# GpSimd takes six eighths of the second payload side beside some units of a bitonic sort, and half beside the others

## The reference, cut to what matters

```python
for i in range(E):                                     # 16 experts
    gate_feature = hidden_states * pe[i] @ gate_w + gate_b
    gate_weight, gate_idx = jax.lax.top_k(gate_feature, K)       # K = 384 of 768
    gate_weight = jax.nn.softmax(gate_weight, axis=-1)
    gathered = jnp.take_along_axis(hidden_states, gate_idx, axis=-1)
    y = y + _moe_mlp(gathered * gate_weight, eg_w[i], eu_w[i], ed_w[i])
```

## Time and profile before

| | us | |
|---|---|---|
| median of 3 runs | 6788.27 | 6777.15 to 6796.1 |
| the profiled execution | 6784.21 | span 6782.4 |
| TensorE matmul busy | 5769.8 | 85% |
| VectorE busy | 5283.0 | 78% |
| GpSimd busy | 3697.6 | 55% |
| ScalarE busy | 2751.2 | 41% |

### The profile page before, as it was taken

How to read it: one execution, slowest core, us unless ns; L and a number is a source line. 1 busy time by engine, 2 the same in 40 slices (tenths; PEclk the granted TensorE clock), 3 DMA queues, 4 the chain that set the end, 5 groups by cost and what they waited for, 6 DMA issues and landing times. The chain is left out here.

```text
span 6782.4 us, 73995 instructions
## 1 busy us (share of the span) xinstructions
PE 5769.8 (85%) x16753; PEld 3057.5 (45%) x16753; DVE 5283.0 (78%) x6633; ACT 2751.2 (41%) x4419; POOL 3697.6 (55%) x3692
## 2 busy tenths in 40 slices
PE   7979989788888878888888888888888888889988
PEld 5545545344444444444444444444444444445554
DVE  3012002499999999999999999999999999998840
ACT  0000000245555545454545454545454555554431
POOL 2325015265766656565656565656565656666630
PEclk9989999899999999999999999999999999999989
DMA  3356238100000000000000000000000000001001
GB/s 89 106 139 179 101 110 196 41 15 16 20 15 15 14 15 14 15 14 15 14 15 14 15 14 15 14 23 6 29 0 29 14 15 14 15 28 35 15 35 51
DMA packets 118084, 261.01 MB, mean 38 GB/s; under 512 B 39164, under 2 KB 49922, under 8 KB 117682
## 3 DMA queue, kind: packets, MB, share of 16 engines
q1 hardware_dynamic: 70322, 180.18, 7.5%
q0 software_dynamic: 47360, 77.17, 5.1%
HBM read 222.43 MB, written 34.58 MB: 38 GB/s over the span
## 5 line engine op out<-in xcount | busy, mean ns | idle before, releaser
L1204 PE MATMUL mask_ps<-key,neg_ident 125*125 125x480 f32 (+7 forms) x4128 | 1884.8, 575 | 599.4 <-DVE key L1612 596.1
L1493 ACT COPY mask_ps<-key 125x960 f32<-125x960 f32 (+7 forms) x1152 | 955.0, 829 | 1733.8 <-DVE pay L1652 1072.8
L1313 POOL TENSOR_TENSOR pay<-pay_side,pay 125x480 int32<-125x480 int32 (+5 forms) x1120 | 1102.2, 984 | 882.9 <-DVE pay L1635 878.4
L1204 PEld LDWEIGHTS mask_ps<-key,neg_ident 125*125 125x125 f32 x4128 | 726.9, 192 | 1503.0 <-DVE key L1612 1048.3
L1305 POOL TENSOR_TENSOR pay_side<-pay 125x480 int32<-125x480 int32 (+5 forms) x1120 | 1098.0, 980 | 481.6 <-DVE pay L1652 346.5
L1635 DVE COPY_PREDICATED pay<-mask_ps,pay 125x960 f32<-125x960 int32 (+6 forms) x1120 | 1236.5, 1104 | 53.3 <-PE mask_ps L1204 29.1
L1602 DVE TENSOR_TENSOR key<-mask_ps,key 125x960 f32<-125x960 f32 (+6 forms) x1120 | 1089.8, 973 | 48.8 <-PE mask_ps L1204 38.4
L1612 DVE TENSOR_TENSOR key<-mask_ps,key 125x960 f32<-125x960 f32 (+6 forms) x1120 | 1089.6, 973 | 0.0
L1204 PE MATMUL mask_ps<-key_top,neg_ident 125*125 125x480 f32 (+3 forms) x1472 | 609.2, 543 | 184.6 <-DVE key_top L1612 170.8
L1652 DVE COPY_PREDICATED pay<-mask_ps,pay_side 125x480 f32<-125x480 int32 (+5 forms) x1120 | 710.6, 634 | 4.8 <-DVE pay L1635 2.9
L1151 PE MATMUL slot_ps<-w_exp,hid 128*125 128x384 f32 x1920 | 685.9, 496 | 9.4 <-issue 9.4
(11 more groups left out here) (190 smaller groups left out, 5855.9 us busy)
## 6 DMA issues: line engine op xcount, KB each, us to landing
w_rel<-L_gnn_W SPq DMA_DIRECT2D x16, 2304.0 KB, 23.3
w_exp<-L_ffn_ed_w SPq DMA_DIRECT2D x16, 2304.0 KB, 8.4
messages_dram<-y_out SPq DMA_DIRECT2D x16, 1875.0 KB
w_exp<-L_ffn_eg_w SPq DMA_DIRECT2D x16, 1152.0 KB, 5.4
w_exp<-L_ffn_eu_w SPq DMA_DIRECT2D x16, 1152.0 KB, 7.8
root_w<-L_gnn_root SPq DMA_DIRECT2D x2, 2304.0 KB
w_exp<-L_ffn_sg_w SPq DMA_DIRECT2D x4, 1152.0 KB, 5.9
w_exp<-L_ffn_su_w SPq DMA_DIRECT2D x4, 1152.0 KB, 8.7
```

The costliest lines, as they stand in the source:

```text
L1204: last = pe.matmul(mask, neg_ident[0:TP, 0:TP], operand, start=False, stop=True, skip_group_check=True)
L1313: pool.tensor_tensor(second, shares(pay_was(turn, u), turn, u)[1].bitcast(I32), first, ALU.subtract).then_inc(pays_taken, 1)
L1493: act.copy(seed_of(turn, u), compared(turn, u)[0]).then_inc(seeded, 1)
```

## The change

`shares` gives GpSimd 6/8 instead of 4/8 of the second side in those units of `REGULAR` that are in the set `turn.free`. The set is computed from the schedule of the loop's turns: units in which GpSimd has no `weigh` and nothing of the list that `beside_all` gives it with a lag of 2. The same set holds in all 15 turns of `REGULAR`, also in the first and the last, whose lists of other work are different. Units from `streams` on stay at 3/8, `OPENING` and `CLOSING` as they were. No instruction is added, removed or reordered; in each unit whose cut moves, the add and the take of GpSimd become longer, and VectorE's second copy and ScalarE's saving copy become shorter.

```diff
@@ -126,6 +126,7 @@
     def __init__(self, units, streams, first, earlier=None, times=1):
         self.units, self.n, self.streams, self.first = units, len(units), streams, first
         stages = [s for s, _, _ in units]
+        self.free = set()
         self.joint = [stages.index(s) for s in JOINT if s in stages]
@@ -199,7 +200,7 @@
     dim = next(d for d in range(1, len(view.shape)) if view.shape[d] > 1)
-    eighths = 4 if u < turn.streams else 3
+    eighths = 3 if u >= turn.streams else 6 if turn is REGULAR and u in turn.free else 4
     cut = view.shape[dim] - max(1, view.shape[dim] * eighths // 8)
@@ -1055,6 +1056,19 @@
+        def asked(flag, parts):
+
+            return do if flag else nothing, ([],) if flag else (), parts
+
+        asked_early = [asked(True, parts) for parts in down_parts(KD)]
+        asked_early += [asked(half == 1 and t + 2 < NT, parts) for t, half, parts in halves_of(gate_parts, range(AHEAD))]
+        asked_late = [asked(False, parts) for parts in turn_parts]
+        asked_late += [asked(n % 2 == 1, parts) for n, parts in enumerate(mixed_parts(KK, KD))]
+        asked_late += [asked(False, parts) for _, _, parts in halves_of(gate_parts, range(AHEAD, NT))]
+        asking = beside_all(REGULAR, asked_early, asked_late, 2)
+        REGULAR.free = {u for u in range(REGULAR.n) if not WEIGH <= u < WEIGH + NT
+                        and all(work is nothing for work, _ in asking.get(u, []))}
```

## The result

| | before | after |
|---|---|---|
| median of the runs, us | 6788.97 (6777.15 to 6796.1, 4 runs) | 6723.94 (6713.35 to 6737.39, 4 runs) |
| profiled execution, us | 6784.21 | 6728.35 (span 6726.6) |
| mean of the loop's 13 turns, us | 324.67 | 320.61 |

The ratio is 0.9908, with a 95% interval of 0.9892 to 0.9925: the change makes the kernel 65 us faster. The forecast was 91 us (6697 us, in a range of 6656 to 6755). The direction and the mechanism held; a good quarter of the gain is missing, and the experiments look for it. The two profiled executions stand 55.9 us apart. 52.9 us of that come from the 13 loop turns (4.07 us each), 1.1 from turn 1, 4.4 from turn 15 and what follows; 2.5 us are lost because the sorts start that much later.

The account below looks back on a forecast made before the run. VectorE was taken as the bound. Its 8.77 us a turn, less 0.77, 0.77, 0.37, 0.50 and 0.15, left 6.21, 80.7 us in 13 turns; with 5 each for turns 1 and 15, 91 us: 6697 us, range 6656 to 6755.

Parts of the forecast that it names:

- What bounds the kernel: In a regular turn of 324.2 us VectorE is the bound, busy 314.9 us, 97%.
- The count and GpSimd's side: 37 of 93 units change; GpSimd pays 32.3 us more a turn, and 720 columns take it about 1.7 us.
- VectorE's saving: Its second copy gets shorter by 1.14 ns a column: 7695 columns, 8.77 us a turn if all showed.
- End of the turn: At unit 90 GpSimd's take, 0.50 us longer, is on the path and VectorE's 0.27 us is lost: 0.77 us.
- Units 39 to 45: Unit 39's longer take heads GpSimd's queue and delays the seed of unit 45: 0.77 us off the saving.
- Unit 75: Unit 74's longer take delays the add that unit 75's first payloads wait for: 0.37 us off the saving.
- Start of the turn: TensorE runs masks and products back to back; waits for masks of units 2 and 7 swallow 0.50 us.
- so this rule stays out of the sum: VectorE's masked copies run beside GpSimd unheld, so whole-instruction exclusion on the shared port pair was given no cost.
- TensorE as bound in the early units: Rival: savings in units 1 to 38 are all lost, a turn gains 3.1 us, 6742 us; chance 0.11.
- Nothing: Rival: GpSimd lands on the path in about 12 places, so nothing to measure, say 6785 us; chance 0.08.
- the slower kernel: Rival: GpSimd's longer add or take comes too late beside busy units, 6931 us if all 27 are hit; chance 0.06.
- The engines exclude each other: Rival: GpSimd's added 32.3 us a turn pushes VectorE by as much, less 8.8: 7141 us; chance 0.01.

Follow-up runs that it names:

- the kernel where GpSimd does not stand in the way, the kernel that beats both: The changed kernel with the negation moved to ScalarE and units 39, 74, 89 and 90 kept at 4/8: 6674.06 us, ratio 0.9830.
- the two kernels of 317.2 us: The changed kernel with GpSimd's old short instructions, some payloads unmoved (6673.4 us); and with the negation on ScalarE, units 39, 74, 89, 90 at 4/8 (6674.06 us).

## Why the prediction was right or wrong

**What bounds the kernel: right.** A turn in which VectorE saves 7.7 us (314.9 to 307.2) is 4.4 us shorter, and 6.8 (324.2 to 317.4) in the kernel where GpSimd does not stand in the way.

**The count and GpSimd's side: right.** 37 units; 30.7 us more a turn (32.3 forecast); 1.65 us for 720 columns (1.7, taken from the slope of the operation's two sizes); adds waited for 1.5 us a turn, under 2.

**VectorE's saving: slightly too large.** By the starts of the units 1.08 ns a column in place of 1.14, 8.3 instead of 8.77 us a turn: 0.46 us.

**The subtracted places.** End of the turn: 0.77 forecast, 0.77 measured (5.20 to 4.43). Units 39 to 45: 0.77 forecast, and 2.70 to 1.69, 1.01, measured, since the seed of unit 44 is late as well. Unit 75: 0.4 to 0.8 as forecast. Start of the turn: 1.35 of savings less 0.50 are 0.85 us by unit 10, measured 0.98 in this short turn and 0.51 in the long one; The prediction has TensorE back to back there. It is so only from unit 3 on; before each of the first three masks of the turn it pauses over 2 us, in before too. Missing: unit 90's mask, where the turn falls back by 0.28 us.

**The step that failed** is "so this rule stays out of the sum". I weighed the port rule on the masked copies only, and for them the trace bears me out: the copy of 240 columns takes 439 ns, while GpSimd is busy three quarters of the turn. I did not go through VectorE's other instructions. One of them, the negation, reads and writes SBUF with one input; it stood in the trace of before at 0.38 us and ended with GpSimd's add. It is held 0.84 us longer in after, 10.9 us in 13 turns. The Trainium skill (SBUF — State Buffer, section Who interferes with whom) lists `tensor_scalar`, which the negation is, among the VectorE operations that can take the port pair shared with GpSimd if their operands meet certain conditions; the engine that issues first keeps the pair for its whole instruction, and the other is blocked. This case agrees: GpSimd's add starts first, and the negation ends 0.02 to 0.03 us behind it in before, in after and in the kernels with unit 38 even and with unit 38 alone. That it is this lock, and not another, is read from the ends and from the Trainium skill, not measured apart.

**An assumption I never wrote down** was that TensorE's clock stays as it is. The seven long turns, less the shorter first one, put after's mean 0.8 us above the 319.8 of the short ones; before's falls put its mean 0.4 above its steady 324.2; 0.4 net.

**The sum by turn:** 6.21 forecast and 4.07 measured, 2.14 short; by these terms 0.84 (held) + 0.46 (a column's price) + 0.24 (seeds) + 0.28 (unit 90's mask) + 0.4 (clock) = 2.2. The remaining differences nearly cancel. These are losses read one by one from the traces of before and after. They aren't what a repair brings: the negation taken off VectorE brought 0.26 us. In 13 turns 28 us; turn 1 gained 1.1 instead of 5 us, turn 15 4.4 of 5, and 2.5 are lost before the sorts. That is 35 of the 35 us between 91 and the 55.9 of the profiled executions; the medians stand 9 us further apart. I can't say why turn 1 gained so little: its length was a bound's middle, not read from rows.

**The rivals.** TensorE as bound in the early units: false (experiment with the first 39 units). Nothing, and the slower kernel: false for the whole, true for the places on the path, where three units alone cost 29 us. The engines exclude each other: false for the masked copies, true for the one instruction. The price of the clock was in none of them. With it, 50 us are lost to four units and a negation of five elements.

**Open:** why, after the same pause of 2.04 us at unit 55, the clock falls in one turn and not in the next, and why a change at unit 39 bears on it. One difference stands in the trace of after: the long stretch over the turn's border ends 17.2 to 17.4 us into each of the five short turns and 17.7 to 18.5 us into each of the seven long ones. It can't be the whole answer, since in the two kernels of 317.2 us it ends at 17.6 to 18.2 us, behind their first loop turn, and no fall follows. Extra products to keep TensorE busy in the pause were not tried, and neither was a delay that moves VectorE's work without a longer pause of TensorE.

## What to carry to other kernels

Before work goes to an engine with idle time, list the places where its results are waited for and leave these out: here 33 changed units bring 116 us together with a moved negation, and 37 bring 65. Look at every instruction of the relieved engine beside the loaded one, also those of a few elements, and compare its end with the other's end. Where TensorE works between pauses, allow for more than the length of what a change adds to the path: the clock may fall at another place, as it did here 50 us behind the added VectorE instruction (1.0 us a turn for the instruction, 1.6 for the clock). Profile more than one execution before counting such falls.

## What the runs showed of the hardware

- A VectorE negation (`tensor_scalar`) of 5 elements a partition, SBUF to SBUF, takes 0.24 to 1.29 us in before and after, and ends 0.03 us behind a GpSimd add or take that started before it, each time. A reciprocal of 5 elements beside a GpSimd add takes 0.16 to 0.18 us and isn't held. Neither is a masked copy with its mask in PSUM: 480 columns took 0.77 us with a take running beside it, 0.78 us without.
- The same negation takes ScalarE 0.20 us.
- A pause of TensorE of 2.04 us was followed by 2.4 GHz in each loop turn of the kernel that beats both, and by 1.2 GHz for some 3 us in 7 of 13 in after. A pause made 1.1 us longer at one place (0.68 to 1.76 us) moved the kernel by 28 us by the medians of two batches (22 by their ratios), of which the added instruction itself, 1.0 us a turn, is some 15.
- One unit's 210 columns, moved to an engine that is idle a third of the turn, made a kernel of 6790 us slower by 20.
